# Holding four zero fills of DRAM row buffers back until four adjacency loads have landed

## The chip, the cores and the metric

The kernel runs on one core of a Trainium2 chip. The metric is the time of one execution on the device in microseconds (us); lower is better. A separate, profiled execution gives the trace. In it PE is the matrix engine (TensorE), DVE the vector engine, ACT the scalar engine, POOL the GpSimd engine and SP the sync engine; a name with q behind it (SPq, ACTq) is the part of an engine that issues transfers and waits.

## The reference, cut to what matters

The input is x (128 graphs of 64 nodes with 128 features) and adj (128 matrices of 64x64). First a graph layer, then a mixture of eight experts of which each node uses two:

```python
x = x + gnn(layernorm(x), adj)     # the graph layer
x = x + ffn(layernorm(x))          # the experts

# gnn(x): h = layer_norm(x, gamma, beta)
#   return x + relu(einsum('bij,bjh->bih', adj, h) @ W_rel + b_rel + h @ W_root)
# ffn(x): the two best of 8 experts by a gate, softmax of their scores;
#   sum over them of p * (relu(x @ W1[e].T + b1[e]) @ W2[e].T + b2[e])
```

## The kernel before

The 8192 nodes lie in 64 tiles of 128 nodes, and these are worked through in four quarters (q) of 16 tiles. Within a quarter the work goes by quads: four groups (k) of four tiles. Each engine has its own instruction stream, written out by hand in a function of its own, and semaphores order them.

The graph layer of a quarter goes like this. DVE makes the statistics of x (`scales_in`, bn_stats at L384) and the normalized tiles (L402). PE transposes them (L809). ACT copies the transposes out of PSUM with gamma and beta (`hT_copy`, L701). PE multiplies by W_rel (`relation`, L816), and ACT copies that (`u_copy`, L706). PE then does W_root and the adjacency product into one bank per quad (`convolve`, L824 and L825); before quad k it waits on the semaphore `adj_in[k]`, which two loads of 64 KB each raise to 32. DVE adds the bias (L417: one input in PSUM, one in SBUF), applies the relu and adds x (L420: both inputs in SBUF), and takes the statistics (L425). When all four quads are through, it works out the moments (L373 to L377) and normalizes (L429 to L442). Routing follows, and then POOL scatters the rows of the quarter to their experts' places in DRAM (`rows`, L298, indirect transfers). The graph layer of quarters 0 and 1 stands ahead of the expert blocks; that of 2 and 3 is mixed in between them.

A row buffer in DRAM has places that no node fills, so all four buffers (3 MB each, `rows0` to `rows3`) are first filled with zeros from the SBUF tile XB. ACT issues these fills (L669). POOL waits for `zero_out[q]` before it scatters quarter q, and SP waits for all four before it loads the first rows.

The order of issue at the start is this:

- SP: x of quarter 0, the constants, eight loads of ADJ (two for each quad, L223 and L224), w2 into YG[1] (L229, 2 MB), x of quarters 2 and 3 (L231, 1 MB each); then a reload of ADJ after each quad's convolution of quarter 0.
- ACT: w1 into YG[0] (L661, 2 MB), x of quarter 1 (L662, 1 MB), four small loads of biases, the four fills (L669). Then come its computing instructions, in the same stream: `hT_copy`, `u_copy`, and the high halves of the weights (L743, W1H and W2H).
- POOL: it scales w1 and w2 in place when each has landed (L283), then makes the low halves (L286): W1L after W1H, W2L after W2H. Each of these works on 128x4096 elements.

```python
for n, (w, s) in enumerate(((YG[0], W1S), (YG[1], W2S))):
    pool.wait_ge((w1_in, w2_in)[n], 16)
    nc.gpsimd.tensor_scalar(w[:, :], w[:, :], s, 1.0, ALU.mult, ALU.mult).then_inc(scaled, 1)
for n, (w, hi, lo) in enumerate(((YG[0], W1H, W1L), (YG[1], W2H, W2L))):
    pool.wait_ge(whi_made, n + 1)
    nc.gpsimd.tensor_tensor(lo[:, :], w[:, :], hi[:, :], ALU.subtract).then_inc(wlo_made, 1)
```

Of the kernel before, what the change touches and what calls it, by code (L numbers as in the profile page):

```python
# [19 lines left out]
NG = TQ // GT  # L37
# [22 lines left out]
def build(nc, x, adj, wrel, wroot, wg, w1, w2, b1, b2, kf, kh, out):  # L60
    ctx = ExitStack()
    with ctx:
# [6 lines left out]
        def sem(name):  # L69
            return ctx.enter_context(nc.semaphore(name))  # L70
# [90 lines left out]
        adj_zero, adj_in = sem("adj_zero"), [sem(f"adj_in{k}") for k in range(NG)]  # L161
# [494 lines left out]
        def _(act):  # L656
# [6 lines left out]
            for r in (0, 32):  # L663
                act.dma_start(B1F[r:r + 4, :], b1[:, :]).then_inc(b_in, 16)
                act.dma_start(B2F[r:r + 1, :], b2[:, :]).then_inc(b_in, 16)
            for q in range(Q):

                n = NR * P // (2 * LW)
                act.dma_start(rows_p[q].rearrange("p (n c) -> p n c", n=n),  # L669
                              ZERO.unsqueeze(1).to_broadcast([P, n, 2 * LW])).then_inc(zero_out[q], 16)  # L670
# [339 lines left out]
```

## Time and profile before

| | |
|---|---|
| time, median of 3 runs | 629.91 us |
| lowest and highest | 625.02 and 630.95 us |
| span of the profiled execution, first to last instruction | 878.1 us |
| the profiled execution's time outside that span | not recorded |
| DVE / PE / POOL / ACT busy in the span | 385.6 / 471.1 / 272.6 / 237.7 us |
| first stretch of the span in which the transfer engines are full | to about 57 us |

The profiled execution is 248 us longer than the timed ones. So a duration read in the trace stands for the timed run only where the stretch in question isn't one of those that grow under the profiler. The change lies in the first 75 us of the span.

### The profile page before, as it was taken

How to read it: one execution, taken by the hardware profiler on the slowest of the kernel's cores; microseconds unless marked ns; L12 is line 12 of the kernel's file. 1: busy time of each engine (PE TensorE's matmuls, PEld its weight loads, DVE VectorE, ACT ScalarE, POOL GpSimd, SP SyncE). 2: the span in 40 equal slices, each digit the busy share in tenths (PEclk: the TensorE clock that was granted, in tenths of full speed). 3: DMA queues.
4: the chain of work that ended last, by engine and by line, in shares of the span. 5: the costliest groups of instructions: out<-in, count | busy, mean ns of one | idle time of the engine just before them, and what ended most of it. 6: DMA issues, size and time to landing. Idle time of an engine off the chain costs nothing.

```text
span 878.1 us, 14976 instructions
## 1 busy us (share of the span) xinstructions
PE 471.1 (54%) x4776; PEld 395.1 (45%) x4777; DVE 385.6 (44%) x1146; ACT 237.7 (27%) x467; POOL 272.6 (31%) x268
## 2 busy tenths in 40 slices
PE   0613243441799997401099997201299951899500
PEld 0613233330688886201088886100188840688400
DVE  2979933830454667200044668000055620456622
ACT  0413100210356554000056553000044410344200
POOL 3053373067000000777400001777300067000274
PEclk9955575565799999655589999655599975899955
DMA  9980012011112112211112112111122222221341
GB/s 346 416 287 1 19 51 64 6 58 51 43 44 78 56 57 67 68 54 51 33 44 78 57 57 82 52 54 51 27 73 72 72 78 53 74 73 54 135 132 57
DMA packets 32173, 70.78 MB, mean 81 GB/s; under 512 B 14458, under 2 KB 14714, under 8 KB 31364
## 3 DMA queue, kind: packets, MB, share of 16 engines
q1 hardware_dynamic: 21520, 37.66, 13.0%
q0 software_dynamic: 8192, 16.79, 6.6%
q10 hardware_dynamic: 2420, 15.77, 4.4%
q8 instruction: 27, 0.44, 0.2%
q14 instruction: 14, 0.11, 0.0%
HBM read 32.45 MB, written 37.75 MB: 80 GB/s over the span
## 4 chain that ended last, share of the span: by engine, by line
PE 42%; issue 20%; another core or an unknown queue 13%; DVE 13%; DMA 4%; ACT 3%; POOL 3%; SPq 2%; ACTq 0%; DVEq 0%; POOLq 0%
PE PH L876 14%; PE PY L893 13%; PE PH L872 5%; POOL YG L311 3%; DMA ADJ<-in_adj 3%; PE PX L859 2%; ACT N L695 1%; PE PY L886 1%; SPq L223 1%; ACT N L677 1%; PE PA L824 1%; DVE VARN L377 1%; DVE MDIF L376 1%; DVE N L442 1%
## 5 line engine op out<-in xcount | busy, mean ns | idle before, releaser
L298 POOL DMA_INDIRECT rows<-XHL,IDX x128 | 123.2, 962 | 347.1 <-DVE IDX L515 309.3
L540 DVE SCALAR_TENSOR_TENSOR HL<-PH,HH 128x512 f16<-128x512 f32 x192 | 129.8, 689 | 207.0 <-ACT HH L726 114.1
L726 ACT ACTIVATE HH<-PH 128x512 f16<-128x512 f32 x192 | 113.6, 596 | 263.1 <-PE PH L876 107.9
L311 POOL DMA_INDIRECT YG<-yrows,IDX x128 | 121.3, 948 | 202.7 <-DMA yrows<-YB 164.3
L876 PE MATMUL PH<-XT,W1H 128*128 128x256 f16 x768 | 144.3, 281 | 22.8 <-issue 22.6
L893 PE MATMUL PY<-W2H,HL 128*128 x768 | 131.0, 223 | 31.8 <-issue 31.8
L893 PE MATMUL PY<-W2H,HH 128*128 x768 | 131.1, 223 | 25.3 <-issue 25.3
L893 PE MATMUL PY<-W2L,HH 128*128 x768 | 109.3, 223 | 42.1 <-issue 42.1
L535 DVE COPY XT<-PX 128x512 f16<-128x512 f16 x96 | 40.5, 422 | 168.6 <-issue 63.1
L876 PE MATMUL PH<-XT,W1L 128*128 128x256 f16 x384 | 107.8, 281 | 12.3 <-issue 12.3
L876 PEld LDWEIGHTS PH<-XT,W1H 128*128 x768 | 76.3, 100 | 55.8 <-issue 32.9
L893 PEld LDWEIGHTS PY<-W2H,HL 128*128 128x128 f16 x768 | 76.4, 99 | 34.1 <-issue 32.7
L893 PEld LDWEIGHTS PY<-W2H,HH 128*128 128x128 f16 x768 | 76.4, 100 | 29.0 <-issue 27.8
L872 PE MATMUL PH<-KH,B 128*128 128x512 f16 x192 | 76.0, 396 | 19.3 <-issue 17.0
L732 ACT ACTIVATE YB<-PY 128x256 f32<-128x256 f32 x96 | 36.7, 382 | 163.1 <-remote 91.2
L893 PEld LDWEIGHTS PY<-W2L,HH 128*128 128x128 f16 x768 | 60.4, 99 | 44.7 <-issue 44.7
L859 PE MATMUL PX<-KH,XB 128*128 128x128 f16 x384 | 39.8, 225 | 31.8 <-issue 19.6
L550 DVE SCALAR_TENSOR_TENSOR X<-YG,PR,X 128x128 f32<-128x128 f32 (+1 forms) x128 | 36.1, 346 | 31.3 <-DMA YG<-yrows,IDX 31.0
L876 PEld LDWEIGHTS PH<-XT,W1L 128*128 x384 | 38.6, 100 | 18.7 <-issue 13.6
L859 PEld LDWEIGHTS PX<-KH,XB 128*128 128x128 f16 x384 | 27.3, 102 | 36.1 <-issue 30.2
L872 PEld LDWEIGHTS PH<-KH,B 128*128 x192 | 19.1, 99 | 26.8 <-issue 24.7
L886 PE MATMUL PY<-B,KH 128*128 x96 | 26.9, 280 | 0.8 <-issue 0.7
(154 smaller groups left out, 559.8 us busy)
## 6 DMA issues: line engine op xcount, KB each, us to landing
rows<-XB ACTq DMA_DIRECT2D x4, 3072.0 KB, 29.8
XB<-rows SPq DMA_DIRECT2D x32, 384.0 KB
yrows<-YB SPq DMA_DIRECT2D x32, 384.0 KB, 2.3
out<-X SPq DMA_DIRECT2D x16, 256.0 KB
X<-in_x SPq DMA_DIRECT2D x3, 1024.0 KB, 28.2
YG<-in_w ACTq DMA_DIRECT2D x1, 2048.0 KB, 9.6
ADJ<-in_adj SPq DMA_DIRECT2D x32, 64.0 KB, 3.8
YG<-in_w SPq DMA_DIRECT2D x1, 2048.0 KB, 29.7
```

The source lines that it names most:

```text
L298: nc.gpsimd.indirect_dma_start(rows[q], bass.IndirectOffsetOnAxis(ap=IDX[:, col:col + 1], axis=0), XHL[:, src:src + 2 * P].bitcast(F32), N ...
L311: nc.gpsimd.indirect_dma_start(YG[q % 2][:, dst:dst + P], None, yrows[q], bass.IndirectOffsetOnAxis(ap=IDX[:, col:col + 1], axis=0)).then_ ...
L535: nc.vector.tensor_copy(XT[:, j % 2 * 2 * BW:(j % 2 + 1) * 2 * BW], PX[:, 0:BW].bitcast(F16)).then_inc(xT_made[j], 1)
L540: nc.vector.scalar_tensor_tensor(HL[:, at:at + 2 * BW], PH[h][:, :], 0.0, HH[:, at:at + 2 * BW], ALU.max, ALU.subtract).then_inc((loa_made ...
L550: ins = nc.vector.scalar_tensor_tensor(xv, y, cols(PR, (q * 2 + e) * TQ + i * GT + k, 1), xv, ALU.mult, ALU.add)
L726: nc.scalar.activation(HH[:, at:at + 2 * BW], PH[h][:, :], ACT.Relu).then_inc((hia_made, hib_made)[h][j], 1)
L732: nc.scalar.mul(YB[:, j * BW:(j + 1) * BW], PY[j % 2][:, 0:BW], 1.0 / YS).then_inc(y_made[j], 1)
L859: last = nc.tensor.transpose(px[:, s * BW + t * P:s * BW + (t + 1) * P], src[:, s * P:(s + 1) * P], ident16)
L872: nc.tensor.matmul(ph[:, :], cols(B1, e, P), KH[:, H_B1M + h * 2 * BW:H_B1M + (h + 1) * 2 * BW], start=True, stop=False, skip_group_check= ...
L876: last = nc.tensor.matmul(ph[:, c % 2 * BW:(c % 2 + 1) * BW], cols(w, e * C + c * P, P), v, start=False, stop=(c % 2 == 1 and w is W1L), s ...
L886: nc.tensor.matmul(py[:, 0:BW], KH[:, H_B2M:H_B2M + P], cols(B2, e, P).unsqueeze(1).to_broadcast([P, 2, P]), start=True, stop=False, skip_ ...
L893: last = nc.tensor.matmul(py[:, t * P:(t + 1) * P], h[:, at:at + P], cols(w, e * C + c * P, P), start=False, stop=(c == C - 1 and w is W2L ...
```

## The change

ACT now waits for all four semaphores `adj_in[0]` to `adj_in[3]` (both loads of each quad landed) before the first fill. Nothing else is changed: the same transfers, the same streams, the same number of instructions but for the waits. (The other lines of the diff take blank lines out at the top of the file; line numbers of the changed kernel are smaller by 17 above the edit and by 15 behind it.)

```diff
             for r in (0, 32):
                 act.dma_start(B1F[r:r + 4, :], b1[:, :]).then_inc(b_in, 16)
                 act.dma_start(B2F[r:r + 1, :], b2[:, :]).then_inc(b_in, 16)
+            for k in range(NG):
+                act.wait_ge(adj_in[k], 32)
             for q in range(Q):
 
                 n = NR * P // (2 * LW)
```

## Rows read from the trace of the kernel before

**Rows 1.** The page: span, and two lines of the busy slices (22 us each).

```profile
span 878.1 us, 14976 instructions
...
DMA  9980012011112112211112112111122222221341
GB/s 346 416 287 1 19 51 64 6 58 51 43 44 78 56 57 67 68 54 51 33 44 78 57 57 82 52 54 51 27 73 72 72 78 53 74 73 54 135 132 57
```

**Rows 2.** Chain that ended last, 0 to 82 us: start, length, what.

```profile
21.05 27.19 DMA ADJ<-in_adj
...
52.05 0.70 DVE TMP L417
...
54.60 3.50 DVE VARN L374
...
58.23 7.82 DVE MDIF L376
...
66.08 7.86 DVE VARN L377
```

**Rows 3.** Timeline of POOL: start, length, instruction, idle time before it.

```profile
13.54 3.61 POOL L283 TENSOR_SCALAR YG<-YG 128x4096 f32<-128x4096 f32 x1 [7.91 <-DMA YG<-in_w]
54.46 3.61 POOL L283 TENSOR_SCALAR YG<-YG 128x4096 f32<-128x4096 f32 x1 [37.31 <-DMA YG<-in_w]
58.04 7.96 POOL L286 TENSOR_TENSOR W1L<-YG,W1H 128x4096 f16<-128x4096 f32 x1
65.97 7.92 POOL L286 TENSOR_TENSOR W2L<-YG,W2H 128x4096 f16<-128x4096 f32 x1
101.29 1.18 POOL L298 DMA_INDIRECT rows<-XHL,IDX  x1 [27.40 <-DVE IDX L515]
```

**Rows 4.** Timeline of ACT.

```profile
26.16 1.28 ACT L701 ACT_TABLE_LOAD   x1 [26.16 <-PE PH L809]
27.45 1.45 ACT L701 ACTIVATE T<-PH,KF 128x512 f32<-128x512 f32 x2
...
33.73 0.59 ACT L706 COPY U<-PY 128x512 f32<-128x512 f32 x1 [0.31 <-PE PY L816]
34.22 3.61 ACT L743 CAST W1H<-YG 128x4096 f16<-128x4096 f32 x1
```

**Rows 5.** Line L669, third and fourth fill: ns to issue; us to landing.

```profile
L669 ACTq DMA_DIRECT2D rows<-XB x2: 4597/7141/9685, 8.3 to 12.9; - x2
...
DMA to landing us min/median/max: 33.4/38.0/42.7
```

**Rows 6.** Transfers of ACT's queue, 22.57 to 60 us, 20 to 50 us: packets, MB.

```profile
q10 hardware_dynamic: 1702, 10.06, 64.3%
...
q10 hardware_dynamic: 1791, 10.70, 85.2%
```

**Rows 7.** Transfers of SP's queue, 20 to 50 us, and 24.69 to 80 us.

```profile
q1 hardware_dynamic: 1811, 1.90, 17.8%
...
q1 hardware_dynamic: 4006, 5.05, 28.2%
```

**Rows 8.** Timeline of SP's issues.

```profile
12.89 4.20 SPq L224 DMA_DIRECT2D ADJ<-in_adj  x1
17.13 3.88 SPq L223 DMA_DIRECT2D ADJ<-in_adj  x1
```

**Rows 9.** ADJ loads of 250 to 420 us, alone on the queues.

```profile
L223 SPq DMA_DIRECT2D ADJ<-in_adj x4: 634/642/652, 250.6 to 332.2; - x4
...
DMA to landing us min/median/max: 2.4/2.6/3.1
```

**Rows 10.** Line L816 on PE: ns of one; from 28.5 and from 31.5 us.

```profile
L816 PE MATMUL PA<-WREL,T x8: 421/421/422, 28.9 to 30.4; 128*128 128x128 f32 x8
...
L816 PE MATMUL PY<-WREL,T x16: 275/275/275, 31.7 to 33.4; 128*128 128x128 f32 x16
```

**Rows 11.** Timeline of DVE.

```profile
16.54 3.19 DVE L384 BATCH_NORM_STATS2 ST<-X 128x6 f32<-128x128 f32 x16 [16.54 <-DMA WG<-in_wg]
...
39.11 0.69 DVE L417 TENSOR_TENSOR TMP<-PH,KF 128x512 f32<-128x512 f32 x1
39.84 0.69 DVE L420 SCALAR_TENSOR_TENSOR X<-TMP,X 128x512 f32<-128x512 f32 x1
...
41.47 0.69 DVE L417 TENSOR_TENSOR TMP<-PH,KF 128x512 f32<-128x512 f32 x1
```

**Rows 12.** Windows: length; busy us of PE, PEld, DVE, ACT, POOL; clock; DMA.

```profile
475.00:500.00 25.00, 24.32 (x281) 21.66 (x280) 14.77 (x44) 14.15 (x30) 0.00 (x0) 1.00 0.22 68
...
575.00:600.00 25.00, 2.38 (x9) 0.94 (x9) 0.69 (x1) 0.60 (x1) 18.90 (x21) 0.50 0.18 52
```

## The prediction

> **What bounds the kernel now.** I read the page first: the transfer engines are full for the first 57 us and then hardly used [rows 1]. So I went to the chain of waits of that stretch. It shows two things. The chain stands 27.19 us on ADJ: the last two loads land at 48.2 us, PE does the last quad, and DVE starts on it at 52.05 [rows 2]. And then three tiny DVE instructions on 16 columns take 3.50, 7.82 and 7.86 us [rows 2]. POOL's timeline explains them: in just these stretches POOL scales w2 (54.46, 3.61 us) and makes W1L (58.04, 7.96 us) and W2L (65.97, 7.92 us), and each DVE instruction ends when POOL's does [rows 2, 3]. DVE gets through at 73.9 us. That is the number to follow: everything later (the routing, POOL's first scatter at 101.29 [rows 3], quarter 1, the expert blocks) hangs on DVE's work of quarter 0, and the fills are needed only at that scatter, over 40 us after they have landed.
>
> The profiled execution is longer than the timed ones by 248 us. Where POOL issues indirect transfers, PE's busy time falls from 24.32 to 2.38 us in 25 [rows 12]; the excess lies there, some ten such stretches, and not in the first 75 us. So I take the first 75 us of the trace at face value, and carry what is gained there to the end one to one: 629.91 minus the gain.
>
> **The change, part by part.**
>
> *ADJ lands early.* Now the two queues take turns: from 20 to 50 us ACT's queue moved 1791 packets and SP's 1811 [rows 6, 7], but these carried 10.70 MB (fills) and 1.90 MB. A 256-byte packet of ADJ waits behind a 6 KB packet of a fill each time. Without fills behind w1 and x of quarter 1, SP's queue runs free from 16 us on. The sixth ADJ load is being issued then; two more at 0.64 us each [rows 8, 9] are out by about 17.5, and land 2.4 to 3.1 us after their issue [rows 9]: about 20.0 us instead of 48.2.
>
> *w2 comes early too.* It is next in SP's stream, then x of quarters 2 and 3. Its scaling on POOL (3.61 us) falls to about 26 to 30 us, where DVE is going to wait for other things anyway. This takes the 3.50 us of L374 off DVE's path.
>
> *ACT is held.* This is the price. ACT's computing instructions stand behind the fills in its stream. Before, the fourth fill took 9.7 us to issue [rows 5] because the queue was full; it was through at 22.57 us, before ACT's first work at 26.16 [rows 4], so it cost nothing. A fill is 528 packets (512 of data, 16 to signal), four are 2112. When the fourth was accepted, 1702 packets (10.06 MB) were still to move [rows 6], so some 410 packets, 2.5 MB, must have left before ACT is free. After the change the fills start from an empty queue at 20.0; three go in at about 0.63 us each, the fourth must wait until 410 packets have moved. Data starts 1.7 us after issue (estimate: 2.4 us to landing less the transfer), so at 21.7. By then w2 has had 2.2 us: 0.9 of 2.1 MB at 416 GB/s [rows 1]. Left on SP's queue are 1.2 MB of w2 and 2.1 MB of x, in packets that now take turns with the fills': some 370 against 410. So all of it moves in this time: 3.3 + 2.5 = 5.8 MB, at 416 GB/s 14.0 us. ACT is free at 35.7 instead of 22.6 us, and its first work starts 9.5 us later than at 26.16. The cover (waiting for DVE and PE) is gone.
>
> The bounds of that: if the queue accepts all four at once, ACT is free at 22 and loses nothing. SP's own queue holds less: when the eighth ADJ load was accepted at 24.69, 4006 packets moved from then on, of which 2608 belong to later issues (w2 144, x 288, eight reloads of 272), so 1398 were outstanding [rows 7]. With that limit on ACT's queue 714 packets (4.3 MB) must leave first: 18.2 us, free at 39.9. I take 35.7, since it is the same queue with the same packets.
>
> *From ACT to DVE.* Table load 1.28 us, then four copies of 0.72 (1.45 for two) [rows 4]: 37.0 to 39.8. PE's relation follows the first copy at 37.7. The matrix engine has been idle since about 29, so I expect its lower clock at first: before, a matmul of L816 took 421 ns at 28.9 us and 275 at 31.7, after PE had worked for 6 us [rows 10]; a quad took 1.7 us at first and 1.0 then. Three and a half quads at the slow level and the rest at the fast one give 44.3, the last `u_copy` ends at 44.9 to 45.2, and the copy to W1H starts at 45.2 instead of 34.22 [rows 4]. It takes 3.61 us, so W1L on POOL runs 48.8 to 56.8 and W2L 56.8 to 64.7 (ACT makes W2H from 48.8 to 52.4, in time for it).
>
> DVE gets quad 0 at about 46.6 and does its L417 and L420 by 48.0, just ahead of W1L. It then does quad 1's L417, and is caught at its L420 until 56.8; it does that, the statistics and quad 2's L417, and is caught again until 64.7. What is left: that L420 0.7, statistics 0.95, quad 3 at 2.36 (from L417 to L417, 39.11 to 41.47 [rows 11]), moments 0.8 (five instructions of 0.1 to 0.2 us). Sum 69.5, against 73.9 before. **Gain 4.4 us.** Each us that ACT is freed later or earlier moves this by one, and at 40.1 us the gain is used up.
>
> *Which DVE instruction is caught.* A row bears on this: bn_stats at 16.54, with one input, ran at its usual 0.28 us beside POOL's scaling of w1 (13.54 to 17.15) [rows 3, 11], while the two-input ones on 16 columns were held. No row shows L417 (one input in PSUM) beside POOL. If it was held as well, quad 1's L417 would wait for W1L and its L420 for W2L; left would be 0.7 + 0.95 + 2 x 2.36 + 0.8, DVE through at 71.9, a gain of 2.0. I take 4.4, as bn_stats is the nearer row. The Trainium skill (SBUF — State Buffer, Who interferes with whom) says that a DVE instruction with two SBUF inputs contends with a GpSimd one that reads SBUF, and one with at most one SBUF input outside the two-port modes doesn't; by that rule L417 goes free and the sum is the 4.4 above.
>
> *The clock.* The granted clock of the stretch before 31.1 us is recorded as full, but the 421 ns are 1.5 times the 275 of later [rows 10], which speaks for the lower level. With the full level throughout, the relation would end 2.5 us sooner and the gain be 6.9. The Trainium skill (TensorE: Matmul & The Clock Gate, Part 1: The HAM clock gate) has the lower level as the default that activity releases; that would keep it at 4.4.
>
> *The end of the fills.* The bytes are the same and the engines stay full but for about 1 us, so the fills end at 57 to 59 us as before; the first scatter asks for them at about 97. Reloads of ADJ start later (from 47 us) and are needed after 95. No cost.
>
> **The rivals.**
>
> 1. *ACT isn't held*: the queue, empty when the fills come, takes all four. Then L743 stands where it was, W1L runs 37.8 to 45.8 and W2L to 53.7; DVE is caught twice in the end of `scales_in(1)` and after that has 1.0 of it, four quads (9.4) and the moments (0.8) to do: 64.9, gain 9.0, **620.9 us**. For it: the packets of the limit may be counted otherwise than I do. Against it: both queues were seen full at under 1750 packets, and four fills are 2112.
>
> 2. *Slower: the fills are accepted later.* If ACT's queue holds only two fills beside what is moving, 1056 packets (6.3 MB) must leave, and with the 3.3 MB that is 23.1 us: ACT free at 44.8, loss 4.7, **634.6 us**. It decides from 40.1 us on; for a loss over 1% ACT would have to be held to 46.4. For it: SP's queue held 1398 only. Against it: 1702 in [rows 6].
>
> 3. *Nothing comes through*: the 4 us are won at 74 us and given back, because POOL's scatters or the PE phases in the timed run hang on something else: 629 to 631 us. I see nothing in the trace that starts at a fixed time after 60 us, but the trace is 248 us away from the timed run there.
>
> 4. The wait does nothing, because ADJ lands before the fills' first packets anyway: excluded, it lands at 48.2.
>
> **How the numbers follow.** Forecast 625.5 us (629.91 minus 4.4), chance 0.5, which takes in 2.0 to 6.9 us of gain (623.0 to 627.9). ACT's queue at SP's limit (gain 0.2, 629.7) 0.13; rival 1 0.12; rival 2 0.08; rival 3 0.15; the rest, other things, 0.02. 1% is 6.3 us, about what a measurement of this kernel can tell from no change. Faster by over 1% are rival 1 and the upper edge of the forecast, 0.24; slower by over 1% needs rival 2 beyond its price or a low draw of the runs before, 0.1; within 1% the remaining 0.66. The range leaves out rival 2 and the outer half of rival 1: 620.0 to 632.0.
>
> **What would show it.** ADJ's last landing near 20 us; the fourth fill's issue ending near 36; the table load at about 36 instead of 26.16; the scaling of w2 at 26 to 27; W1L from 48 to 50 us; two L420 of about 8 us and no long instruction in L373 to L377; L429 at 69 to 70 instead of 73.96; the first scatter at 97. The prediction is wrong if the fourth fill's issue ends before 30 or after 40, if DVE is caught at three places, or if a gain at 74 us doesn't appear in the time.

## The result and the profile after

| | before | changed |
|---|---|---|
| time, median of 4 runs each | 628.02 us | 622.02 us |
| lowest and highest | 625.02 and 630.95 | 620.04 and 622.87 |
| ratio, 95% interval | | 0.9899 (0.9856 to 0.9942) |
| span of the profiled execution | 878.1 us | 621.0 us |

The change makes the kernel faster by 1.0%, and the interval doesn't reach 1. The forecast was 625.5 us with a range of 620.0 to 632.0.

The two spans can't be compared as they stand: chips of two kinds turned up in this study. On one kind the kernel before takes 625 to 631 us, on the other 878 to 888 us, profiled or not, so each kernel below is compared only with the kernel before of its own job (a group of runs on one chip). By its span of 878.1 us, the trace of the kernel before is from a chip of the second kind. The 248 us aren't the profiler's, as the prediction had it; the last section shows the rows. The first 75 us are alike on both: the changed kernel was traced on each kind, and DVE starts L412 at 67.60 and at 67.89 us. There the two traces answer each other. The ratios in this document leave out two far slower executions (916 and 1214 us).

The timeline of ACT in the changed kernel, where the prediction sees the price:

```profile
19.97 14.94 ACTq L654 DMA_DIRECT2D rows<-XB  x4
35.00 1.28 ACT L686 ACT_TABLE_LOAD   x1 [35.00 <-issue]
...
42.93 3.61 ACT L728 CAST W1H<-YG 128x4096 f16<-128x4096 f32 x1
46.44 3.61 ACT L728 CAST W2H<-YG 128x4096 f16<-128x4096 f32 x1
```

The four fills are issued from 19.97, when ADJ's last load has landed, and ACT is free at 34.91. Its table load moves from 26.16 to 35.00, and W1H from 34.22 to 42.93 [rows 4].

The timeline of POOL:

```profile
24.89 3.69 POOL L266 TENSOR_SCALAR YG<-YG 128x4096 f32<-128x4096 f32 x1 [7.57 <-DMA YG<-in_w]
46.62 7.95 POOL L269 TENSOR_TENSOR W1L<-YG,W1H 128x4096 f16<-128x4096 f32 x1 [18.04 <-ACT W1H L728]
54.54 8.37 POOL L269 TENSOR_TENSOR W2L<-YG,W2H 128x4096 f16<-128x4096 f32 x1
94.94 1.18 POOL L281 DMA_INDIRECT rows<-XHL,IDX  x1 [32.03 <-DVE IDX L498]
```

The scaling of w2 comes at 24.9 instead of 54.5, the low halves 11.4 us earlier, and the first scatter at 94.94 instead of 101.29 [rows 3].

The timeline of DVE in the same stretch (start, length, instruction, idle time before it):

```profile
24.01 7.47 DVE L385 TENSOR_SCALAR N<-X,SCI,SHI 128x128 f32<-128x128 f32 x16
...
44.31 0.69 DVE L400 TENSOR_TENSOR TMP<-PH,KF 128x512 f32<-128x512 f32 x1 [1.67 <-PE PH L810]
...
46.67 0.69 DVE L400 TENSOR_TENSOR TMP<-PH,KF 128x512 f32<-128x512 f32 x1
47.39 7.73 DVE L403 SCALAR_TENSOR_TENSOR X<-TMP,X 128x512 f32<-128x512 f32 x1
...
56.07 0.69 DVE L400 TENSOR_TENSOR TMP<-PX,KF 128x512 f32<-128x512 f32 x1
56.79 6.67 DVE L403 SCALAR_TENSOR_TENSOR X<-TMP,X 128x512 f32<-128x512 f32 x1
...
67.60 0.17 DVE L412 TENSOR_SCALAR RA<-VARN 128x16 f32<-128x16 f32 x1
...
76.83 3.19 DVE L367 BATCH_NORM_STATS2 ST<-X 128x6 f32<-128x128 f32 x16
```

The instruction that started at 73.96 before (L429, now L412) starts at 67.60. This is 6.36 us earlier, and where they come from can be added up. DVE's idle time fell from 5.89 us (before the last quad, up to 52.05 [rows 2]) to 1.67 us (the row at 44.31): 4.2 us. Its holds by POOL fell from 3.4 + 7.6 + 7.7 = 18.7 us (each long instruction of [rows 2] less its usual 0.2) to 3.3 (sixteen L385 took 7.47 instead of 4.19) + 7.0 + 6.0 (the two long L403 less their usual 0.69) = 16.3: 2.4 us. The start of it all was 0.3 later. 4.2 + 2.4 - 0.3 = 6.3.

### The profile page after: what moved, and what is told of

The parts are those of the page before. It is cut to its first block, busy times and chain, and to the rows that moved or that the text cites. A ratio compares the mean times of both kernels' runs of the same rounds, so it can differ in the third digit from the quotient of the medians.

```text
span 621.0 us, 14978 instructions
## 1 busy us (share of the span) xinstructions
PE 438.9 (71%) x4776; PEld 384.6 (62%) x4777; DVE 383.8 (62%) x1146; ACT 237.6 (38%) x467; POOL 274.7 (44%) x268
## 3 DMA queue, kind: packets, MB, share of 16 engines
q1 hardware_dynamic: 21520, 37.66, 18.6%
## 4 chain that ended last, share of the span: by engine, by line
PE 59%; DVE 17%; issue 7%; POOL 6%; ACT 3%; ACTq 3%; DMA 2%; SPq 2%; DVEq 0%; POOLq 0%
PE PH L861 19%; PE PY L878 18%; PE PH L857 7%; POOL YG L294 6%; PE PX L844 3%; DVE X L403 3%; ACTq L654 2%; PE PY L871 1%; ACT N L662 1%; PE PB L801 1%; PE PA L809 1%; PE PA L810 1%; PE PA L822 1%; DVE ST L408 1%; DVE ST L367 1%
## 5 line engine op out<-in xcount | busy, mean ns | idle before, releaser
L281 POOL DMA_INDIRECT rows<-XHL,IDX x128 | 124.9, 976 | 211.5 <-DVE IDX L498 173.7
L861 PE MATMUL PH<-XT,W1H 128*128 128x256 f16 x768 | 140.8, 279 | 0.0
L878 PE MATMUL PY<-W2H,HH 128*128 x768 | 127.5, 220 | 0.0
L878 PE MATMUL PY<-W2H,HL 128*128 x768 | 127.3, 220 | 0.0
L878 PE MATMUL PY<-W2L,HH 128*128 x768 | 105.8, 219 | 0.0
L878 PEld LDWEIGHTS PY<-W2H,HH 128*128 128x128 f16 x768 | 75.2, 98 | 1.2
L717 ACT ACTIVATE YB<-PY 128x256 f32<-128x256 f32 x96 | 36.7, 382 | 77.5 <-PE PY L878 76.6
L878 PEld LDWEIGHTS PY<-W2L,HH 128*128 128x128 f16 x768 | 59.0, 98 | 0.0
L844 PE MATMUL PX<-KH,XB 128*128 128x128 f16 x384 | 38.1, 223 | 18.0 <-DVE XT L518 17.3
L844 PEld LDWEIGHTS PX<-KH,XB 128*128 128x128 f16 x384 | 26.5, 101 | 19.9 <-DVE XT L518 11.5
L794 PE MATMUL PH<-KF,N 128*128 128x128 f32 x16 | 4.3, 430 | 36.4 <-DVE N L385 36.4
```

Source lines behind the costliest of these rows:

```text
L281: nc.gpsimd.indirect_dma_start(rows[q], bass.IndirectOffsetOnAxis(ap=IDX[:, col:col + 1], axis=0), XHL[:, src:src + 2 * P].bitcast(F32), N ...
L717: nc.scalar.mul(YB[:, j * BW:(j + 1) * BW], PY[j % 2][:, 0:BW], 1.0 / YS).then_inc(y_made[j], 1)
L844: last = nc.tensor.transpose(px[:, s * BW + t * P:s * BW + (t + 1) * P], src[:, s * P:(s + 1) * P], ident16)
L861: last = nc.tensor.matmul(ph[:, c % 2 * BW:(c % 2 + 1) * BW], cols(w, e * C + c * P, P), v, start=False, stop=(c % 2 == 1 and w is W1L), s ...
L878: last = nc.tensor.matmul(py[:, t * P:(t + 1) * P], h[:, at:at + P], cols(w, e * C + c * P, P), start=False, stop=(c == C - 1 and w is W2L ...
```

## The experiments

There were four more jobs, each on one chip with the kernel before beside the others. Beside the times one place in the traces is used as a yardstick: the start of the third block of sixteen bn_stats (`scales_in(2)`), which DVE does when the graph layer of quarter 0 is finished. It is at 83.2 us in the kernel before and at 76.8 in the changed one.

One thing blurs it. DVE's first bn_stats waits for the load of WG (4 KB), and this lands at another time in every trace: 16.54 us in the kernel before, 16.83 and 17.10 in the two traces of the changed kernel, and 11.70 to 17.36 in all the kernels in which SP issues the ADJ loads before w2 and ACT no fill before 19 us. The table at the end of this section has this start beside the yardstick. The edits are shown against the changed kernel where nothing else is said; lines that are left out are marked.

### The changed kernel again

No edit.

> The changed kernel itself, on the same chip and beside the kernel before as the three that follow, as their base. Theory A (what counts is when DVE is through with quarter 0, since nothing later has a time of its own): 6 us less than the kernel before, ratio 0.990, with L412 at 67.6 us. Rival (the gain was a draw of the runs): a ratio that includes 1.

Measured: 881.5 us against 885.14 for the kernel before in this job; ratio 0.9966 (0.9946 to 0.9986). L412 starts at 67.89 and the yardstick is at 77.12, both 0.3 after the first trace. The gain is there, but 3.6 us and not 6; the interval (1.2 to 4.8 us) leaves out the 6.1 us that DVE is early. So on this chip something is lost behind 77 us, and that part isn't explained.

### The fills behind ACT's casts

```diff
-            for k in range(NG):
-                act.wait_ge(adj_in[k], 32)
-            for q in range(Q):
-
-                n = NR * P // (2 * LW)
-                act.dma_start(rows_p[q].rearrange("p (n c) -> p n c", n=n),
-                              ZERO.unsqueeze(1).to_broadcast([P, n, 2 * LW])).then_inc(zero_out[q], 16)
...
                         nc.scalar.copy(hi[:, :], w[:, :]).then_inc(whi_made, 1)
+                    n = NR * P // (2 * LW)
+                    for r in range(Q):
+                        act.dma_start(rows_p[r].rearrange("p (n c) -> p n c", n=n),
+                                      ZERO.unsqueeze(1).to_broadcast([P, n, 2 * LW])).then_inc(zero_out[r], 16)
```

> The waits are gone, and ACT issues the four fills behind the copies to W1H and W2H of quarter 0, so that ACT is never held before its computing work and the fills take nothing from ADJ, w2 or x. Theory A with POOL's hold (every us that POOL works on the weights while DVE has a two-input instruction next is lost to DVE): W1H starts at about 36.5 instead of 42.9, W1L runs 40 to 48 and W2L 48 to 56; DVE is caught in scales_in(1) with 12.7 us of work behind it, so L412 starts at 68 to 69 and the time is that of the changed kernel or 1 us more (622 to 624). Rival (the 9 us for which ACT is held are the price of the change, and are got back when it isn't): L412 at 60 to 62 us, 616 to 617 us.

Measured: 878.63 against 885.14, ratio 0.9934 (0.9910 to 0.9958), and L412 at 65.6. Both theories missed the place (68 to 69, 60 to 62). The same kernel in the next job:

> The same kernel as fills_behind_casts (fills behind the copies to W1H and W2H), as the base for the one that follows. In its first trace W1L ran 38.6 to 46.6 us, W2L to 54.5, and L412 started at 65.6, 8.3 us before that of the kernel before. If what is won at L412 comes through to the end, 6 to 8 us less than the kernel before; if the 6.5 us of its first timing were a draw, 0 to 4.

Measured: 622.47 against 629.13, ratio 0.9884 (0.9854 to 0.9913), L412 at 68.25, yardstick at 77.5: the place that POOL's hold gives. The 2.6 us between the two traces are there from DVE's start: its first bn_stats is at 14.04 in the first and at 16.77 in the second, and from there to L412 it takes 51.6 and 51.5 us, without idle time. In the changed kernel it is 50.8 in both traces. Here are DVE's long instructions in the second trace:

```profile
23.95 7.52 DVE L385 TENSOR_SCALAR N<-X,SCI,SHI 128x128 f32<-128x128 f32 x16
...
41.17 7.85 DVE L343 SCALAR_TENSOR_TENSOR RT<-RT,RA 128x32 f32<-128x32 f32 x1
49.05 7.85 DVE L344 SCALAR_TENSOR_TENSOR SCI<-RT,SCI 128x32 f32<-128x32 f32 x1
...
68.25 0.17 DVE L412 TENSOR_SCALAR RA<-VARN 128x16 f32<-128x16 f32 x1
```

W1H was made at 37.3 instead of 42.9, and POOL began W1L at 41.0 instead of 46.6. On DVE's path to L412 it bought nothing, since DVE was caught 6 us earlier, and with that much more work behind it. That ACT is held for 9 us isn't what limits the changed kernel up to there. By time this is less clear. In the one job that has both, the kernel with the fills behind the casts took 878.63 us (lowest 875.55, highest 882.02) and the changed one 881.5 (879.13 and 883.66). Some of it can be the earlier start of DVE, and the rest isn't explained.

### Early ADJ without early w2

```diff
-            sp.dma_start(YG[1][:, :], w2[:, :]).then_inc(w2_in, 16)
             for q in range(2, Q):
...
             for k in range(NG):
                 sp.wait_ge(conv_done, k + 2)
+            sp.dma_start(YG[1][:, :], w2[:, :]).then_inc(w2_in, 16)
+            for k in range(NG):
                 load_adj(k, NG + k)
```

> The changed kernel, but SP issues w2 only when the four convolutions of quarter 0 are done (and the reloads of ADJ behind it); ADJ still lands at about 20 us. So this has the early ADJ without the early w2. Theory with POOL's hold: ADJ lets DVE reach L412 at about 53 us, but w2 lands at 58 to 59, POOL works on the weights until 78, and DVE is held at the L425 or L432 that follow until then: L432 of quarter 0 at 78 us (74.4 in the changed kernel, 80.8 before), so 3 to 4 us more than the changed kernel, about 626. Rival (the gain came from ADJ, and w2 is a side effect): as fast as the changed kernel or faster, 610 to 622 us.

> The same kernel as w2_after_convolution (early ADJ, late w2). In its first trace POOL ended W2L at 75.0 us and DVE began L433 at 75.8, 5.0 us before the kernel before (80.8); its time was 5.0 less (880.1 against 885.1), in a job in which the kernel before took 885 us and not 629. If DVE's place at 75 us carries to the end there as here, 624 where the kernel before takes 629. Rival (in a job of 629 us the late w2 matters more): 628 or more.

Measured: 880.12 against 885.14 (ratio 0.9954, 0.9933 to 0.9974), and again 876.11 against 882.15 (0.9926, 0.9900 to 0.9952); both jobs were on chips of the 880 us kind. The yardstick is at 78.2 and 78.1. In the trace of the first, DVE reaches L413 (L412 in the changed kernel, at 67.6) at 50.19, and is then held:

```profile
52.91 22.96 DVE L426 TENSOR_SCALAR N<-X,SCO,SHO 128x128 f32<-128x128 f32 x16
75.79 2.48 DVE L433 SCALAR_TENSOR_TENSOR XHL<-N,XHL 128x512 f16<-128x512 f32 x4
```

POOL worked on w2 and the low halves from 55.5 to 75.0, and sixteen instructions that take 4.2 us took 23.0. So with an ADJ that is early by 28 us DVE comes 24 us ahead. But 18.7 of them are POOL's hold, which has only been put off and comes back here (23.0 less 4.2 is 18.8); what the early ADJ takes away is the 5.9 us of idle time. 5 us are left at the yardstick, 6.1 in the changed kernel of the same job. The early w2 adds about 1 us there. The comparison isn't clean, as without w2 in the queues ACT was free at 29.4 and not at 34.9. The times of the two in the first job, 880.12 and 881.5, overlap and don't order them.

### Early w2 without early ADJ

```diff
+            sp.dma_start(YG[1][:, :], w2[:, :]).then_inc(w2_in, 16)
             sp.wait_ge(adj_zero, 1)
             for k in range(NG):
                 load_adj(k, k)
-            sp.dma_start(YG[1][:, :], w2[:, :]).then_inc(w2_in, 16)
```

> The kernel before, its fills where they were and without any wait, but SP issues w2 ahead of the eight ADJ loads. So this has the early w2 without the early ADJ, which lands a few us later than before (about 52). Theory with POOL's hold: w2 is scaled at 19 to 23 us, W1L runs about 40 to 48 and W2L to 56, DVE is caught in scales_in(1) and finds all convolutions done when it comes out; L412 at about 68, the time of the changed kernel, 622 us. Rival (the gain came from ADJ): no gain or a loss of some 4 us, 628 to 632 us.

> The same kernel as w2_first_only (early w2, late ADJ). First trace: L449 of DVE at 76.9, 3.9 us before the kernel before; time 3.1 less. If that carries to the end, 625 to 626 where the kernel before takes 629. Rival: no gain, 629.

Measured: 882.05 against 885.14 (ratio 0.9959, 0.9937 to 0.9982) and 877.66 against 882.15 (0.9952, 0.9930 to 0.9973), yardstick at 79.3 and 79.1. The fills are where they were, ADJ isn't early, and still the kernel is 3 to 4.5 us faster. (The changed kernel took 881.5 in the first of these jobs: by time it isn't told from either half of itself.) W1L was made from 41.9 and W2L to 57.8, and DVE was held in `scales_in(1)` (7.82 and 7.87 us), while ADJ was still on its way (PE waited for quad 2's until 50.75): the hold and the wait for ADJ lay one on the other. That rules out that the gain is a matter of ADJ alone. Either edit takes away that the two come one after the other.

### DVE makes the low halves

```diff
-            for n, (w, hi, lo) in enumerate(((YG[0], W1H, W1L), (YG[1], W2H, W2L))):
-                pool.wait_ge(whi_made, n + 1)
-                nc.gpsimd.tensor_tensor(lo[:, :], w[:, :], hi[:, :], ALU.subtract).then_inc(wlo_made, 1)
...
                 scales_in(2 * q + 1)
+                if q == 0:
+                    for n, (w, hi, lo) in enumerate(((YG[0], W1H, W1L), (YG[1], W2H, W2L))):
+                        dve.wait_ge(whi_made, n + 1)
+                        nc.vector.tensor_tensor(lo[:, :], w[:, :], hi[:, :], ALU.subtract).then_inc(wlo_made, 1)
```

> The changed kernel, but DVE makes W1L and W2L itself, between scales_in(1) and the residuals of quarter 0, so that POOL does nothing there that could hold it. Estimate from 128x512 in 0.69 us: about 4.4 us each. Theory with POOL's hold: W1H is there at 46.8, W1L to 51.2, W2L to 55.6, four quads and the moments 10.2: L412 at 65.8, 2 us less than in the changed kernel (67.9), 8 less than before. Rival (DVE's long instructions have another cause than POOL, such as the transfers or ACT's casts): instructions of 7 to 8 us stay, and L412 comes at 76 us.

Measured: 621.91 against 629.13, ratio 0.9891 (0.9861 to 0.9922); L409 (the L412 of the changed kernel) at 66.35, yardstick at 75.6. With nothing on POOL no instruction of quarter 0 is long but for L382 beside the scaling of w2, and the two new ones take 4.43 and 4.42 us. That is the plainest proof of the hold: the same arithmetic costs DVE 8.9 us done by itself and 13.0 us done by POOL. But DVE now waits 4.92 us for W1H, because ACT is held; and so the price of the waits shows, as it did not before. With the fills moved behind the casts as well:

> Both edits: fills behind the casts, and W1L and W2L on DVE. Theory with POOL's hold: scales_in(1) ends at 39.9 without a hold, W1L 39.9 to 44.3, W2L to 48.7, then 10.2 us to L412 at 58.9, which is 15 us before the kernel before and 6.7 before fills_behind_casts; time 10 to 15 us less than before. Rival (DVE isn't what later work waits for once it is 9 us early): the time of fills_behind_casts.

Measured: 611.78 against 629.13, ratio **0.9758** (0.9721 to 0.9796). L409 at 58.50 (58.9 expected), yardstick at 67.7.

```profile
24.93 7.54 DVE L390 TENSOR_SCALAR X<-X,SC,SHI 128x128 f32<-128x128 f32 x16
...
39.56 4.43 DVE L558 TENSOR_TENSOR W1L<-YG,W1H 128x4096 f16<-128x4096 f32 x1
43.90 4.42 DVE L558 TENSOR_TENSOR W2L<-YG,W2H 128x4096 f16<-128x4096 f32 x1
58.50 0.17 DVE L409 TENSOR_SCALAR RA<-VARN 128x16 f32<-128x16 f32 x1
```

DVE has no idle time in this stretch, and the kernel takes 10.1 us less than the one before it in the same job: ACT's hold is dear once POOL's is gone. Not all of it is the hold: in this trace DVE started at 11.70 us, 5.0 earlier. What is left of POOL's hold is the 3.3 us in the first row, from the scaling of w2, and 2.0 us further ahead, where an instruction of 0.2 us (L353, at 14.93) took 2.13 beside the scaling of w1.

### No work on the weights on POOL at all

Against the kernel with both edits:

```diff
-            for n, (w, s) in enumerate(((YG[0], W1S), (YG[1], W2S))):
-                pool.wait_ge((w1_in, w2_in)[n], 16)
-                nc.gpsimd.tensor_scalar(w[:, :], w[:, :], s, 1.0, ALU.mult, ALU.mult).then_inc(scaled, 1)
...
-                        nc.scalar.copy(hi[:, :], w[:, :]).then_inc(whi_made, 1)
+                        nc.scalar.activation(hi[:, :], w[:, :], ACT.Copy, scale=s).then_inc(whi_made, 1)
...
-                        nc.vector.tensor_tensor(lo[:, :], w[:, :], hi[:, :], ALU.subtract).then_inc(wlo_made, 1)
+                        nc.vector.scalar_tensor_tensor(lo[:, :], w[:, :], s, hi[:, :], ALU.mult, ALU.subtract).then_inc(wlo_made, 1)
```

> fills_behind_low_on_dve, and the scaling of w1 and w2 leaves POOL too: ACT scales while it makes W1H and W2H, DVE scales while it makes W1L and W2L. Theory with POOL's hold: one tensor_scalar of 128x128 was held 3.3 us by the scaling of w2 (7.5 us for sixteen instead of 4.2); that goes, and L412's place is 55 us instead of 58.5, the time 3 us less than fills_behind_low_on_dve, 608 to 609 where the kernel before takes 629. Rival (the 3.3 us were hidden in a wait that follows): the same time as fills_behind_low_on_dve, 611 to 612.

> The same kernel as no_weight_work_on_pool. If this job is one in which the kernel before takes 629 us: theory (the 3.3 us hold by the scaling of w2 is also got back) ratio 0.966 to 0.971, 608 to 611, against 0.9758 for fills_behind_low_on_dve; rival (it was hidden) 0.974 to 0.977. If it is one of 880 us, the ratio 0.981 of the first timing again, and the two best kernels stay uncompared.

Measured: 864.76 against 882.15 (ratio 0.9814, 0.9789 to 0.9838) and 862.16 against 880.58 (0.9799, 0.9767 to 0.9831). Both are from chips of the 880 us kind, so by time it stays uncompared with the kernel with both edits; in us the two save the same, 17.4 and 18.4 against 17.4. The hold is gone from the trace:

```profile
26.48 4.18 DVE L387 TENSOR_SCALAR X<-X,SC,SHI 128x128 f32<-128x128 f32 x16
...
56.69 0.17 DVE L406 TENSOR_SCALAR RA<-VARN 128x16 f32<-128x16 f32 x1
```

L406 at 56.69 is only 1.8 us ahead of the 58.50, not the 3.3 of the hold. But DVE started at 15.20 here and at 11.70 there. From its start to this instruction it takes 41.5 us against 46.8 (41.5 in the second trace too): 5.3 us less, which is the 3.3 and the 2.0 us of the two scalings. So in the trace nothing of the hold was hidden; whether it all comes through to the time isn't shown.

### Fills in packets of 3 KB

```diff
-                n = NR * P // (2 * LW)
+                n = NR * P // LW
                 act.dma_start(rows_p[q].rearrange("p (n c) -> p n c", n=n),
-                              ZERO.unsqueeze(1).to_broadcast([P, n, 2 * LW])).then_inc(zero_out[q], 16)
+                              XB[:, 0:LW].unsqueeze(1).to_broadcast([P, n, LW])).then_inc(zero_out[q], 16)
```

> The changed kernel with fills cut into runs of 3 KB instead of 6 KB, so the same bytes in twice the packets (4160 against 2112 for the four). Theory that ACT's queue holds some 1700 packets: 2460 of them (7.3 MB) must leave before ACT is free, with 3.3 MB of SP's queue 10.6 MB and 25 us: ACT free at 47 us instead of 34.4, W1L from 59, L412 at 78 to 80 instead of 67.9, the time 6 to 12 us more than the changed kernel, so above the kernel before. Rival (the queue holds a number of bytes or of transfers): ACT free at 34 to 36 and the time of the changed kernel.

Measured: 628.92 against 629.13, ratio 1.0008 (0.9983 to 1.0032). ACT is free at 41.7 us, L412 at 75.2, yardstick at 84.5. Neither theory fits: the fills hold ACT 6.8 us longer than in the changed kernel, not 12 and not 0. DVE is later by 7.6 us at L412, which is the slope of about one to one that the prediction gave to ACT's release, and the gain is used up. Line L654 (ns to issue; first and last start) in this kernel:

```profile
L654 ACTq DMA_DIRECT2D rows<-XB x4: 619/4460/12167, 19.9 to 33.5; - x4
...
DMA to landing us min/median/max: 17.3/25.6/31.0
```

Here the third fill is held as well. From the transfers of the queue that follow such a moment, the packets outstanding can be counted, and what comes nearest to agreeing is the number *ahead* of the transfer that is being accepted:

| transfer accepted | at | outstanding | of these its own | ahead of it |
|---|---|---|---|---|
| fourth fill, before | 22.57 | 1702 | 528 | 1174 |
| fourth fill, changed | 34.91 | 1663 | 528 | 1135 |
| third fill, 3 KB | 33.4 | 2412 | 1040 | 1372 |
| fourth fill, 3 KB | 41.72 | 2312 | 1040 | 1272 |
| eighth ADJ load, before (SP) | 24.69 | 1398 | 272 | 1126 |

Two of the counts, as the trace gives them, ACT's queue from 34.91 us on in the changed kernel and from 41.72 on in this one:

```profile
q10 hardware_dynamic: 1663, 9.82, 52.1%
```

```profile
q10 hardware_dynamic: 2312, 6.96, 44.9%
```

So a transfer went in when some 1130 to 1370 packets of earlier ones were left, on either queue, with packets of 256 bytes, 3 KB and 6 KB. That explains why SP's queue seemed to hold less than ACT's. The fourth fill of the other kernels fits (1149 to 1190 ahead of it in eleven traces), and so do SP's ADJ loads in the kernel before from the sixth on (1095 to 1126). But its fourth and fifth, the first that were held, went in at 861 and 1020, and the 3 KB fills lie above all others; so it isn't one fixed number, and no experiment was made for it.

### All of them in one table

| kernel | DVE's first bn_stats (16.5 before), us | yardstick, us earlier than 83.2 | time, us less than before in its job |
|---|---|---|---|
| 3 KB packets | 16.4 | -1.3 | 0.2 |
| early w2 only | 18.6, 15.5 | 3.9, 4.1 | 3.1, 4.5 |
| early ADJ only | 17.4, 15.9 | 5.0, 5.1 | 5.0, 6.0 |
| changed | 16.8, 17.1 | 6.4, 6.1 | 6.0, 3.6 |
| fills behind casts | 14.0, 16.8 | 8.3, 5.7 | 6.5, 6.7 |
| low halves on DVE | 16.7 | 7.6 | 7.2 |
| both | 11.7 | 15.5 | 17.4 |
| no weight work on POOL | 15.2, 15.6 | 17.2, 16.8 | 17.4, 18.4 |

What DVE wins by 75 us comes out at the end to within 3 us, on both kinds of chip. A yardstick is one trace, a time the median of several runs; so smaller differences in this table say nothing.

## Why the prediction was right

Its path is the one that the traces show: ADJ and w2 early, ACT held, DVE caught by POOL at two L420, a gain that goes through to the end. The gain was 6.0 us instead of 4.4, inside its 2.0 to 6.9. The time itself, 622.02 us, lies below the 623.0 to 627.9 that went with it, since the kernel before came out at 628.02 and not at 629.91.

- *ADJ by 20.0*: it landed at 19.9, and in part by luck: the last load was issued at 13.77 instead of 17 and took 6.1 us instead of 2.4 to 3.1 to land, two misses that cancel.
- *ACT free at 35.7*: 34.91. The sum of bytes holds: from 20 to 35 us SP's queue moved 3.47 MB and ACT's 2.79, together at 418 GB/s. The limit behind it was put wrongly, as 1702 packets in all, which makes no difference for a fill of the same packets. The bound from SP's queue (39.9) was no bound: by the counts above it is the same limit.
- *The scaling of w2 at 26 to 27, harmless*: 24.89. It did hold DVE, for 3.3 us, in a place where the prediction named the cover (DVE waits for PE afterwards). The cover was just large enough, 1.67 us of it being left; in the kernels where DVE has no idle time it costs.
- *W1H at 45.2*: 42.93. This is the term that was off. 0.8 us of the 2.3 come from ACT's release, the rest from the relation on the matrix engine, which took 5.1 us (37.12 to 42.25) instead of 6.6. In L801 (line L816 before) a matmul took 421 ns from 37.12 on and 275 ns from about 40.2, so the slow level held for 3 us of work and not for 6. This varies: in the second trace of the changed kernel the relation took 5.9 us, and in low_halves_on_dve, which is the same kernel up to there, the 6.6 of the prediction. The profile gives the clock of this stretch as full (1.00). That 421 ns mean the lower level all the same is borne out by the last quad of the kernel before, where the same duration stands in a stretch with a granted clock of 0.50 (columns of the first row: length, PE busy, clock, DMA share, GB/s):

```profile
41.40:51.60 10.20, 4.88 (x24) 0.50 1.03 429
```

```profile
L825 PE MATMUL PC<-U,ADJ x8: 274/421/421, 48.9 to 51.7; 128*128 128x128 f32 x8
```

  The Trainium skill (TensorE: Matmul & The Clock Gate, Part 1: The HAM clock gate) says that the default state is the throttled one and activity releases it; the 421 ns after an idle stretch and the 275 ns later agree with that.
- *DVE caught at two L420, not at L417*: as forecast; both L400 (L417 before) took 0.69 us beside POOL's work, and the L403 behind them 7.73 and 6.67.
- *L429 at 69.5, gain 4.4*: 67.60, gain 6.4. 2.3 us of W1H less 0.4 for the last POOL instruction (8.37 against 7.92 us), which probably waited for the end of an L403: this ran until 55.1, and POOL's began at 54.54.
- *Carried to the end one to one*: 6.0 us in the first comparison, but 3.6 in the job of changed_again, where the 6.1 of the trace lie outside the interval; for the others the table above.
- *The rival "ACT isn't held"*: its 620.9 us are nearer to the measured time than the forecast, so the time alone doesn't rule it out; the trace does, as ACT was held 9 us. Its price was wrong too. fills_behind_casts and fills_behind_again take that hold away, and from DVE's start to L412 they take 51.5 us. From the 16.54 of the kernel before this would put L412 at 68.1, where the rival has 64.9: it left out the 3.3 us that the scaling of w2 costs when DVE has no idle time. *The slower rival* (ACT to be held to 40.1 for no gain): the 3 KB kernel tried it, and at 41.7 there is no gain. *That nothing comes through*: out.

## What to carry to other kernels

Before a transfer is moved to make another land early, look at who is next in the queues, and what the engine that issues it has behind it: here the waits cost ACT 9 us, and cost DVE nothing by 75 us only because it was to be held by POOL anyway. When two waits come one after the other on an engine (ADJ, then POOL's hold), removing either gives only what the other doesn't take; the large gain (2.4%) came from removing the work that holds. An instruction that DVE takes 4.4 us for is dear on POOL if it holds DVE for 7.9.

## What the runs showed of the hardware

- **POOL holds DVE for whole instructions, and not only those of DVE with two inputs in SBUF.** A tensor_scalar of 128x128 with one SBUF input took 8.0 us beside W1L (L426 of w2_after_convolution, 333 to 8031 ns) and 3.6 us beside the scaling of w2; bn_stats (0.29 us at 55.17) and the tensor_tensor with one input in PSUM (0.69 us at 56.07) went on beside W2L in the changed kernel. The Trainium skill (SBUF — State Buffer, Who interferes with whom) has tensor_scalar among those that can enter a two-port mode and contend; the trace agrees, and the prediction, which cited the section, had not counted with it for the scaling of w2.

```profile
L426 DVE TENSOR_SCALAR N<-X,SCO,SHO x16: 333/338/8031, 52.9 to 75.5; 128x128 f32<-128x128 f32 x16
```

- **Two kinds of chip.** The stretch of 400 to 425 us, in which POOL issues the same 21 indirect transfers, in the first trace of the changed kernel (621.0 us) and in the second (881.2 us); columns as in [rows 12]:

```profile
400.00:425.00 25.00, 24.17 (x296) 21.35 (x297) 17.04 (x40) 10.66 (x20) 18.90 (x21) 1.00 0.39 118
```

```profile
400.00:425.00 25.00, 3.61 (x19) 2.51 (x20) 0.42 (x1) 2.01 (x6) 18.90 (x21) 0.50 0.20 52
```

On one chip PE runs at full speed beside them, on the other it does 19 instead of 296 matmuls, at a granted clock of 0.50. The other traces fall in the same two groups (9 to 23 matmuls against 269 to 303 in this stretch). In pieces of 5 us, those behind 75 us in which POOL is busy for over 3 us come to 310 us in the changed kernel (621.0 us), with PE busy for 240 of them, and to 315 us in the kernel before, with PE busy for 73. So PE does some 170 us of work less beside POOL, which is most of the 250 us; the rest isn't accounted for. Of the four later jobs one was on a chip of the first kind and three on others of the second. What sets it is open, and so is whether it belongs to the chip or to its state that day.
